# Quarter 3 of the feed-forward weights split in the feed-forward, and the routing's last steps reordered

## The chip, the cores and the metric

The kernel runs on one core of a Trainium2 chip. Its engines work side by side, each with an instruction queue of its own: TensorE (PE), VectorE (DVE), ScalarE (ACT), GpSimd (POOL) and SyncE (SP, which only issues transfers). They wait for each other by semaphores. The metric is the device time of one execution in microseconds.

## The reference

Two layers on `x` (4 batches of 512 rows of 512), each with a residual:

```python
x = x + gat(ctx_512, layernorm(x))                 # graph attention, the normed x as adjacency
x = x + moe(layernorm(x))                          # 8 experts, the best 2 per row, F = 352
x = x + softmax(norm(sim(layernorm(x), ctx @ Wk.T + bk)) * gamma + beta)
h = silu(x_n @ w_gate) * (x_n @ w_up)              # x_n = layernorm(x), I = 2048
x = x + sparsify_2to4(h) @ w_down                  # of every 4 neighbours the 2 largest stay
```

All products keep nearly fp32 precision: each operand is split in a high and a low part, and three products are summed (`product3`, L78 to L80).

## The kernel before

**Routing** (`gat_rows`, the end of its block). Batch by batch TensorE turns the rows (`turn_batch`, L254), multiplies them with the router's weights (`pe_logits`, L281) and counts rows per expert (`pe_count`, L418 and L422; the total is L426). VectorE takes the logits (`dve_logits`), chooses two experts per row (`dve_choose`; `keep`, L395), and behind the last batch makes the places (`dve_places`, from L449), a flag from bounds that TensorE has turned (L1103 to L1112), the token lists (`dve_tokens`, from L507) and the weights of the two experts (`dve_weights`, L435 to L445). GpSimd gathers the first rows (L528), and the block ends with a barrier of all engines.

**Expert stage** (`moe`). The rows come in 39 groups of 128, numbered 0 to 38. `pipeline` runs `body(g, ...)` for g from 1 to 38 on every engine. In a body TensorE makes the gate product of group g, turns the hidden values of g - 1, makes the up product, turns the rows of group g + 1 (L1629), and makes the down product of g - 1. So each L1629 marks one body: that at 154.56 us stands ahead of body 1, and those of bodies 4, 8, 12, 18, 22, 25, 26, 28 and 31 are shown among the rows below. ScalarE's order in a body is silu (L1711), high part of the hidden values (L1715), high part of the turned rows (L1719), result (L1724). Where the table says that a new expert begins soon, its raw weights are split: ScalarE makes the high parts (L1730), VectorE the low ones and the high part of the down weights (L1812, L1856), GpSimd the low part of the down weights (L1577). This happens in bodies 4, 8, 18, 21, 26 and 28.

Beside that work the weights of the feed-forward are split ahead of time. `w_scratch` holds high and low part of 16 rows of weights (4 quarters of 4), and each row is made in two chunks of 768 columns, 32 chunks in bodies 1 to 32. SP loads a raw chunk to one of four places of `pre_raw` (L1554), ScalarE writes its high part to one of two places of `pre` at the end of its body (`chunk_hi`, L1777), GpSimd subtracts (L1583) and issues the store (L1586):

```python
act.wait_ge(pre_kept[j % 2], 32 * i + 16 * (j // 2))     # the store of two chunks before
act.copy(pre[:, j % 2, 0, :], pre_raw[:, j, :]).then_inc(pre_hi, 1)
```

In bodies 29 to 38 the keys of the second layer's attention are made too; ScalarE's first cut stands behind the chunk of body 29 (L1756, L1758), VectorE takes the low part (`kv_c_lo`, L1850), and TensorE's key product stands in body 30.

**Feed-forward** (`ffn`). 16 units n, each one batch and one quarter of the inner width, in an order in which neighbours often share a quarter: `ORDER` gives (batch, quarter), `SPLIT` numbers the loads of a quarter, `FIRST` and `QUARTER` say at which unit a load is first used. Quarter 3 is first used in unit 3 (and again in unit 4, then in 9 and 14). Unit n has slots 6n to 6n + 5. In slots r = 0 to 3 TensorE makes gate and up of row r (`pe_gate_up`), in 4 and 5 the down product of unit n - 1 (`pe_down`). GpSimd fetches split weights from `w_scratch` to `f_w` (`fetch_gate_up` L1384, `fetch_down` L1393). ScalarE makes the silu (L1430), VectorE the product (L1436) and the choice of two in four (`keep_two`, L2650 to L2666), and both serve the attention of the other batches, whose steps `later_plan` sets into slots: `late` is the norm (L2014), `pre` and `post` are VectorE's part.

## Time and profile before

| | |
|---|---|
| median of 3 runs | 1042.15 us (1039.57 to 1042.34) |
| profiled execution | 1042.56 us, its span 1040.8 us |
| mean granted TensorE clock | 0.957 |
| busy share of the span | PE 92%, DVE 62%, ACT 38%, POOL 35% |
| moved | 195.56 MB, 188 GB/s |

The span runs from the first to the last instruction. A share of busy time is a mean over stages; TensorE's matmuls are pipelined. The chain is the work followed back from the last instruction, at each step to what released it. A timeline shows start, duration, engine, line, operation and, in brackets, how long the engine was idle before it and who ended that.

### The profile page before, as it was taken

The numbers are of one execution on the slowest core, as the hardware profiler recorded it, in microseconds if no ns is written. First come the engines' busy times: TensorE is split into PE (matmuls) and PEld (weight loads), VectorE is DVE, ScalarE is ACT, GpSimd is POOL, SyncE is SP. The second block draws the span as 40 slices with busy tenths as digits, with TensorE's granted clock in tenths as the row PEclk, the third lists the DMA queues.
The fourth block names the chain that finished last, engine by engine and source line by source line (L and its number), as shares of the span: only waits on it lengthen the run. The fifth ranks groups of instructions, "written<-read, shape, count | busy, mean of one in ns | idle before, by whom it ended". The sixth has DMA issues, their size and how long they took to land.

```text
span 1040.8 us, 15251 instructions
## 1 busy us (share of the span) xinstructions
PE 960.0 (92%) x4778; PEld 819.8 (79%) x4778; DVE 642.8 (62%) x1429; ACT 392.4 (38%) x697; POOL 360.4 (35%) x441
## 2 busy tenths in 40 slices
PE   4999639999989989858999999999999999999997
PEld 3889639889978888747788888888888888888885
DVE  7988644342432654465795876867858957665446
ACT  4875525444543533332332332422333324222121
POOL 0467026676576754733041220321311311101120
PEclk8998559999999999988999999999999999999999
DMA  9477349887789845364474334664263642545651
GB/s 340 168 147 162 121 132 339 315 305 279 250 304 325 296 178 158 101 207 149 160 238 167 102 111 152 215 222 130 68 216 122 202 162 81 171 154 163 201 146 57
DMA packets 68946, 195.56 MB, mean 188 GB/s; under 512 B 8176, under 2 KB 8304, under 8 KB 67632
## 3 DMA queue, kind: packets, MB, share of 16 engines
q0 software_dynamic: 41392, 129.78, 39.3%
q1 hardware_dynamic: 27456, 64.60, 17.8%
q8 instruction: 45, 0.74, 0.3%
q14 instruction: 53, 0.43, 0.1%
HBM read 146.38 MB, written 50.60 MB: 189 GB/s over the span
## 4 chain that ended last, share of the span: by engine, by line
PE 67%; DVE 6%; DMA 4%; issue 3%; POOL 3%; ACT 2%; DVEq 0%; ACTq 0%; POOLq 0%
PE ps L78 22%; PE ps L80 21%; PE ps L79 21%; DMA w_scratch<-pre 4%; POOL dn_w_lo L1577 2%; PE ps L1629 1%; PE ps L1989 1%; DVE gu_w_lo L1812 1%; POOL pre L1583 1%; DVE raw L2650 1%; PE ps L1657 1%; DVE raw L2666 1%; DVE dn_w_hi L1856 0%; ACT gu_w_hi L1730 0%; DVE m_hT_lo L1805 0%
## 5 line engine op out<-in xcount | busy, mean ns | idle before, releaser
L78 PE MATMUL ps<-f_x_lo,f_w 128*128 128x512 f32 (+1 forms) x524 | 203.2, 388 | 3.3 <-DVE raw L1436 1.7
L80 PE MATMUL ps<-f_x_hi,f_w 128*128 128x512 f32 (+1 forms) x524 | 202.3, 386 | 0.0
L79 PE MATMUL ps<-f_x_hi,f_w 128*128 128x512 f32 (+1 forms) x524 | 202.3, 386 | 0.0
L1430 ACT ACTIVATE moe_rows<-ps 128x512 f32<-128x512 f32 x64 | 38.3, 598 | 221.8 <-PE ps L80 221.7
L1436 DVE TENSOR_TENSOR raw<-moe_rows,ps 128x512 f32<-128x512 f32 x64 | 43.8, 685 | 120.1 <-PE ps L80 112.5
L78 PEld LDWEIGHTS ps<-f_x_lo,f_w 128*128 128x128 f32 x524 | 99.5, 190 | 23.5 <-DVE f_x_lo L2341 2.1
L80 PEld LDWEIGHTS ps<-f_x_hi,f_w 128*128 128x128 f32 x524 | 99.4, 190 | 19.5
L78 PE MATMUL ps<-gu_w_lo,m_xT_hi 128*128 (+1 forms) x312 | 106.0, 340 | 9.5 <-issue 5.7
L79 PEld LDWEIGHTS ps<-f_x_hi,f_w 128*128 128x128 f32 x524 | 99.5, 190 | 19.3
L78 PE MATMUL ps<-f_w,kv_c_hi 128*128 128x512 f32 x256 | 101.8, 398 | 2.3 <-DVE x L2685 2.3
L79 PE MATMUL ps<-gu_w_hi,m_xT_lo 128*128 (+1 forms) x312 | 101.9, 327 | 0.0
L80 PE MATMUL ps<-gu_w_hi,m_xT_hi 128*128 (+1 forms) x312 | 101.9, 327 | 0.0
L79 PE MATMUL ps<-f_w,kv_c_lo 128*128 128x512 f32 x256 | 101.1, 395 | 0.0
L80 PE MATMUL ps<-f_w,kv_c_hi 128*128 128x512 f32 x256 | 101.0, 395 | 0.0
L1805 DVE TENSOR_TENSOR m_hT_lo<-ps,m_hT_hi 128x384 fp32r<-128x384 f32 x39 | 21.7, 555 | 115.1 <-ACT m_hT_hi L1715 106.4
L1393 POOL DMA_DIRECT2D f_w<-w_scratch x52 | 37.0, 715 | 131.0 <-PE ps L80 130.2
L1384 POOL DMA_DIRECT2D f_w<-w_scratch x52 | 38.0, 732 | 116.6 <-PE ps L80 110.7
L1583 POOL TENSOR_TENSOR pre<-pre_raw,pre 128x768 fp32r<-128x768 f32 x32 | 58.9, 1840 | 44.6 <-ACT pre L1777 44.5
L78 PEld LDWEIGHTS ps<-gu_w_lo,m_xT_hi 128*128 128x128 f32 x312 | 59.7, 191 | 15.9 <-issue 9.3
L2685 DVE TENSOR_TENSOR x<-ps,x 128x512 f32<-128x512 f32 x64 | 42.8, 684 | 40.4 <-PE ps L80 40.4
L2650 DVE TENSOR_TENSOR raw<-kv_c_raw 128x768 bf16<-128x768 f32 (+2 forms) x96 | 60.3, 683 | 2.1 <-ACT kv_c_raw L2577 2.1
L79 PEld LDWEIGHTS ps<-gu_w_hi,m_xT_lo 128*128 128x128 f32 x312 | 60.1, 193 | 0.4
(368 smaller groups left out, 2007.3 us busy)
## 6 DMA issues: line engine op xcount, KB each, us to landing
f_w<-w_scratch POOLq DMA_DIRECT2D x52, 1024.0 KB, 5.7
f_w<-w_scratch POOLq DMA_DIRECT2D x52, 512.0 KB, 4.8
w_scratch<-pre POOLq DMA_DIRECT2D x32, 768.0 KB
pre_raw<-in_ffn SPq DMA_DIRECT2D x32, 384.0 KB
raw<-in_moe_gu SPq DMA_DIRECT2D x32, 352.0 KB
y_scratch<-m_y SPq DMA_DIRECT2D x39, 256.0 KB
raw<-in_moe_dn SPq DMA_DIRECT2D x24, 256.0 KB
x<-in_x SPq DMA_DIRECT2D x4, 1024.0 KB, 11.7
```

What stands on the lines that cost most here:

```text
L78: eng.matmul(out, lhs_hi, rhs_lo, start=start, stop=False)
L79: eng.matmul(out, lhs_lo, rhs_hi, start=False, stop=False)
L80: return eng.matmul(out, lhs_hi, rhs_hi, start=False, stop=stop)
L1384: pool.dma_start(self.w[r][:, :, 0:2, :], self.store[RQ * QUARTER[s] + r, :, :, 0:2, :]).then_inc(self.got_gu[r], 16)
L1393: pool.dma_start(self.w[r][:, :, k, :], self.store[RQ * QUARTER[s] + r, :, :, 2, :]).then_inc(got[r], 16)
L1430: act.activation(sg[:, k % 2, :], self.gate_bank(n, r), ACT.Silu).then_inc(self.silu, 1)
L1436: dve.tensor_tensor(out, sg[:, k % 2, :], self.up_bank(n, r), ALU.mult).then_inc(self.hid_made, 1)
L1577: pool.tensor_tensor(rt["dn_w_lo"][:, at], rt["raw_dn"], rt["dn_w_hi"][:, at].bitcast(F32), ALU.subtract).then_inc(dn_lo, 1)
L1583: pool.tensor_tensor(pre[:, k, 1, :], pre_raw[:, j, :], pre[:, k, 0, :].bitcast(F32), ALU.subtract).then_inc(pre_lo, 1)
L1805: dve.tensor_tensor(hT_lo[:, k, :, :], HB.rearrange("p (r n) -> p r n", r=RE), hT_hi[:, k, :, :].bitcast(F32), ALU.subtract).then_inc(h_lo ...
L2650: ins = dve.tensor_tensor(beats[:, at:at + w, :], mag[:, i, :].unsqueeze(1).broadcast_to([P, w, HN]), mag[:, j0:j1, :], ALU.is_ge)
L2685: dve.tensor_tensor(X[:, t, :], u.acc(n, i), X[:, t, :], ALU.add).then_inc(u.acc_free, 1)
```

## The change

In the routing, batch 2 is turned ahead of count 0, and counts 1 to 3 come behind the last logits. The softmax weights are scaled per batch (`dve_scale`), three times in `dve_places` ahead of the wait for the total and once behind it; `limits` (the flag) goes ahead of the last batch's logits, and `dve_weights` ahead of `dve_tokens`. In the expert stage 24 chunks remain, quarters 0 to 2, in the bodies of `SPLITS`. Quarter 3 is split in the feed-forward in six pieces: SP loads raw weights to one of three stages, ScalarE copies the high part straight to `f_w`, VectorE subtracts, and SP stores the pair to `w_scratch` for the later uses. The gate and up pieces stand in slots 1 to 4 of unit 2, the down pieces in slots 1 and 2 of unit 4. GpSimd no longer fetches quarter 3 for units 3 and 4. ScalarE's piece stands behind `late` in its slot (in slot 4 behind `size`), VectorE's behind `post` (in slot 4 at the unit's end).

```diff
-CHUNKS, CW = 2 * Q * RQ, 3 * D // 2
+CHUNKS, CW = 2 * RQ * (Q - 1), 3 * D // 2
+FRESH = (Q - 1,)
...
+    def dve_scale(self, chain, c):
+
+        dve, link = chain.eng, chain.link
+        s = slice(TB * c, TB * c + TB)
+        dve.wait_ge(self.exped, c + 1)
+        link(dve.tensor_tensor(self.ex[:, s, :], self.keep[:, s, :], self.ex[:, s, :], ALU.mult))
+        link(dve.tensor_reduce(self.den[:, s], self.ex[:, s, :], AX.X, ALU.add))
+        link(dve.reciprocal(self.den[:, s], self.den[:, s]))
+        dve.tensor_tensor(self.tw[:, s, :], self.ex[:, s, :], self.den[:, s].unsqueeze(2).broadcast_to([P, TB, E]),
+                          ALU.mult).then_inc(self.scaled, 1)
...
-        dve.wait_ge(self.exped, B)
-        link(dve.tensor_tensor(self.ex[:, :, :], self.keep[:, :, :], self.ex[:, :, :], ALU.mult))
-        link(dve.tensor_reduce(self.den[:, :], self.ex[:, :, :], AX.X, ALU.add))
-        link(dve.reciprocal(self.den[:, :], self.den[:, :]))
-        link(dve.tensor_tensor(self.tw[:, :, :], self.ex[:, :, :], per_e(self.den[:, :]), ALU.mult))
+            ins = dve.tensor_tensor(at[:, :, :], at[:, :, :], self.pos2[:, :, k].unsqueeze(2).broadcast_to([P, T, E]),
+                                    ALU.is_equal)
+        link(ins)
+        dve.wait_ge(self.scaled, B)
...
+        for c in range(B - 1):
+            self.dve_scale(chain, c)
         dve.wait_ge(self.counted, 1)
...
+                turn_batch(2)
+                lo.pe_logits(pe, 2)
                 rank.pe_count(pe, 0)
                 pe.wait_ge(bounds_ready, 1)
                 for j in range(4):
                     ins = pe.transpose(BOUNDS[:, P * j:P * j + P], per_part[:, j:j + 1], ident[:, :])
                 ins.then_inc(bounds_turned, 1)
-                turn_batch(2)
-                lo.pe_logits(pe, 2)
-                rank.pe_count(pe, 1)
                 turn_batch(3)
                 lo.pe_logits(pe, 3)
-                rank.pe_count(pe, 2)
-                rank.pe_count(pe, 3)
+                for c in range(1, B):
+                    rank.pe_count(pe, c)
                 rank.pe_index(pe)
...
+                    if c == B - 1:
+                        limits()
                     lo.dve_logits(dve, c)
                     rank.dve_choose(chain, c)
                 rank.dve_places(chain)
-                dve.wait_ge(bounds_turned, 1)
-                dve.tensor_reduce(red[:, 0:1], BOUNDS[:, 0:P], AX.X, ALU.min)
-                dve.tensor_reduce(red[:, 1:3], BOUNDS[:, P:3 * P].rearrange("p (k n) -> p k n", k=2), AX.X, ALU.add)
-                link(dve.tensor_reduce(red[:, 4:8], BOUNDS[:, 3 * P:4 * P].rearrange("p (k n) -> p k n", k=4), AX.X,
-                                       ALU.max))
-                link(dve.tensor_reduce(red[:, 8:10], red[:, 4:8].rearrange("p (k n) -> p k n", k=2), AX.X, ALU.add))
-                link(dve.tensor_tensor(red[:, 1:3], red[:, 1:3], red[:, 8:10], ALU.mult))
-                link(dve.tensor_scalar(red[:, 3:5], red[:, 1:3], BOUND_MAX, None, ALU.is_le))
-                link(dve.tensor_tensor(red[:, 3:4], red[:, 3:4], red[:, 4:5], ALU.mult))
-                link(dve.tensor_tensor(red[:, 3:4], red[:, 3:4], red[:, 0:1], ALU.mult))
-                dve.tensor_copy(flag[:, :], red[:, 3:4])
+                rank.dve_scale(chain, B - 1)
+                rank.dve_weights(chain)
...
+    def pieces(n, slot):
+
+        down = (("down", n - 1, slot - 1),) if n - 1 in FRESH and slot <= RQ // 2 else ()
+        gate_up = (("gate_up", n + 1, slot - 1),) if n + 1 in FRESH else ()
+        return down + gate_up
...
+    def load_piece(self, sp, piece):
+        kind, s, i = piece
+        at, t = self.place[piece], RQ * QUARTER[s]
+        if at >= 3:
+            sp.wait_ge(self.raw_lo, at - 2)
+        if kind == "gate_up":
+            sp.dma_start(self.stage[at % 3], self.raw[t + i][:, 0:2 * D]).then_inc(self.raw_got[at % 3], 16)
+        else:
+            sp.dma_start(self.piece_stage(piece), self.raw[t + 2 * i:t + 2 * i + 2, :, 2 * D:3 * D].rearrange("r p n -> p r n")
+                         ).then_inc(self.raw_got[at % 3], 16)
+
+    def keep_piece(self, sp, piece):
+        kind, s, i = piece
+        t = RQ * QUARTER[s]
+        sp.wait_ge(self.raw_lo, self.place[piece] + 1)
+        if kind == "gate_up":
+            sp.dma_start(self.store[t + i, :, :, 0:2, :], self.w[i][:, :, 0:2, :].bitcast(F32)).then_inc(self.kept_gu[i], 16)
+        else:
+            for r in (2 * i, 2 * i + 1):
+                sp.dma_start(self.store[t + r, :, :, 2, :], self.w[r][:, :, 2, :].bitcast(F32)).then_inc(self.kept_dn[r], 16)
+
+    def act_piece(self, act, piece):
+        kind, s, i = piece
+        at, stage = self.place[piece], self.piece_stage(piece)
+        act.wait_ge(self.raw_got[at % 3], 16 * (at // 3) + 16)
+        if kind == "gate_up":
+            act.wait_ge(self.products, RQ * (FIRST[s] - 1) + i + 1)
+            act.copy(self.w_hi[i][:, 0:2, :], stage).then_inc(self.raw_hi, 1)
+        else:
+            act.wait_ge(self.acc_done, TB * FIRST[s])
+            for k, r in enumerate((2 * i, 2 * i + 1)):
+                ins = act.copy(self.w_hi[r][:, 2, :], stage[:, k, :])
+            ins.then_inc(self.raw_hi, 1)
+
+    def dve_piece(self, dve, piece):
+        kind, s, i = piece
+        stage = self.piece_stage(piece)
+        dve.wait_ge(self.raw_hi, self.place[piece] + 1)
+        if kind == "gate_up":
+            dve.tensor_tensor(self.w_lo[i][:, 0:2, :], stage, self.w_hi[i][:, 0:2, :].bitcast(F32), ALU.subtract
+                               ).then_inc(self.raw_lo, 1)
+        else:
+            for k, r in enumerate((2 * i, 2 * i + 1)):
+                ins = dve.tensor_tensor(self.w_lo[r][:, 2, :], stage[:, k, :], self.w_hi[r][:, 2, :].bitcast(F32),
+                                         ALU.subtract)
+            ins.then_inc(self.raw_lo, 1)
...
+        SPLITS = {1 + 4 * m // 3: m for m in range(CHUNKS)}
+        LOADS = {g - 3: m for g, m in SPLITS.items() if g > 3}
...
-                if g <= CHUNKS:
-                    split_chunk(g, j, i)
+                if g in SPLITS:
+                    split_chunk(SPLITS[g])
...
+            order = list(u.place)
+            sp.wait_ge(first.sim_done, TB)
+            for piece in order[:2]:
+                u.load_piece(sp, piece)
+            for k, piece in enumerate(order):
+                if k + 2 < len(order):
+                    u.load_piece(sp, order[k + 2])
+                u.keep_piece(sp, piece)
```

Two of the three stages, `fresh_raw`, lie where `kv_wk_raw` and the first key lie before; the third is the end of `raw`. The first loads wait for the first batch's last similarity product.

## Rows read from the trace of the kernel before

**Rows 1.** Windows: length, busy PE, PEld, DVE, ACT, POOL, PEclk, DMA share, GB/s

```profile
148.00:440.00 292.00, 273.38 (x1575) 249.60 (x1575) 116.62 (x173) 126.71 (x227) 180.37 (x198) 0.98 0.75 261
...
516.00:1015.00 499.00, 499.00 (x2255) 411.43 (x2255) 344.69 (x804) 148.41 (x229) 105.29 (x145) 1.00 0.50 158
```

**Rows 2.** The page's chain, shares by engine and line

```profile
PE ps L78 22%; PE ps L80 21%; PE ps L79 21%; DMA w_scratch<-pre 4%; POOL dn_w_lo L1577 2%; PE ps L1629 1%; PE ps L1989 1%; DVE gu_w_lo L1812 1%; POOL pre L1583 1%; DVE raw L2650 1%; PE ps L1657 1%; DVE raw L2666 1%; DVE dn_w_hi L1856 0%; ACT gu_w_hi L1730 0%; DVE m_hT_lo L1805 0%
```

**Rows 3.** Timeline of PE, L1629: bodies 4, 8, 12, 18, 22, 25, 26, 28, 31

```profile
181.34 0.60 PE L1629 MATMUL ps<-ident,moe_rows 128*128 128x128 f32 x4
...
210.79 0.60 PE L1629 MATMUL ps<-ident,moe_rows 128*128 128x128 f32 x4
...
239.25 0.60 PE L1629 MATMUL ps<-ident,moe_rows 128*128 128x128 f32 x4
...
279.52 0.60 PE L1629 MATMUL ps<-ident,moe_rows 128*128 128x128 f32 x4
...
311.21 0.60 PE L1629 MATMUL ps<-ident,moe_rows 128*128 128x128 f32 x4
...
332.98 0.60 PE L1629 MATMUL ps<-ident,moe_rows 128*128 128x128 f32 x4
...
339.65 0.60 PE L1629 MATMUL ps<-ident,moe_rows 128*128 128x128 f32 x4
...
353.14 0.60 PE L1629 MATMUL ps<-ident,moe_rows 128*128 128x128 f32 x4
...
382.36 0.66 PE L1629 MATMUL ps<-ident,moe_rows 128*128 128x128 f32 x4 [0.32 <-DVE k_first L1840]
```

**Rows 4.** Chain behind body 26; ScalarE's waits before L1777; the last one

```profile
345.94 3.50 POOL dn_w_lo L1577
...
349.44 1.82 POOL pre L1583
...
351.55 9.08 DMA w_scratch<-pre
...
  DMA w_scratch<-pre: 17.3, 5
...
360.71 0.83 ACT L1777 CAST pre<-pre_raw 128x768 fp32r<-128x768 f32 x1 [4.25 <-DMA w_scratch<-pre]
```

**Rows 5.** Timeline of PE: the key product of body 30

```profile
370.47 0.50 PE L78 MATMUL ps<-kv_c_lo,kv_wk_hi 128*128 128x512 f32 x1 [2.50 <-DVE kv_c_lo L1850]
```

**Rows 6.** Timelines of PE, DVE and POOL at the end of the routing

```profile
117.88 0.64 PE L418 MATMUL ps<-g_keep,g_before_p 128*128 128x32 f32 x2 [1.11 <-DVE g_keep L395]
...
115.06 0.19 DVE L287 COPY logits<-ps 128x32 f32<-128x32 f32 x1 [3.26 <-PE ps L281]
...
120.65 0.29 DVE L451 TENSOR_TENSOR g_above<-ps,g_steps 128x128 f32<-128x128 f32 x1 [2.25 <-PE ps L426]
...
130.65 0.27 DVE L1103 TENSOR_REDUCE g_red<-ps 1x1 f32<-1x128 f32 x1
...
132.48 0.18 DVE L507 COPY g_tok_sum<-ps 128x39 f32<-128x39 f32 x1
...
135.65 0.27 DVE L445 TENSOR_REDUCE weight<-g_high 128x16 f32<-128x128 f32 x1
...
134.18 1.08 POOL L528 DMA_INDIRECT moe_rows<-xn_scratch,moe_index  x1 [0.17 <-issue]
```

**Rows 7.** Timelines of ACT and DVE in unit 2

```profile
554.77 0.58 ACT L1430 ACTIVATE moe_rows<-ps 128x512 f32<-128x512 f32 x1
...
563.36 1.07 ACT L2577 ACTIVATE kv_c_raw<-raw 128x1024 f32<-128x1024 f32 x1
...
545.79 0.69 DVE L2672 TENSOR_TENSOR kv_c_lo<-raw,kv_c_hi 128x512 fp32r<-128x512 f32 x1
...
555.44 0.69 DVE L1436 TENSOR_TENSOR raw<-moe_rows,ps 128x512 f32<-128x512 f32 x1 [2.64 <-ACT moe_rows L1430]
...
561.76 0.69 DVE L1436 TENSOR_TENSOR raw<-moe_rows,ps 128x512 f32<-128x512 f32 x1 [4.10 <-PE ps L80]
```

More of the change, by code:

```diff
@@ L1360, in __init__ @@
         self.acc_done, self.acc_free = sem(tag + "acc_done"), sem(tag + "acc_free")
+        self.raw = outer["dram"]["ffn"]
+        self.stage = [outer["raw"][:, 4 * D:6 * D]] + [outer["fresh_raw"][:, k, :] for k in range(2)]
+        self.raw_got = [sem(f"{tag}raw_got{k}") for k in range(3)]
+        self.raw_hi, self.raw_lo = sem(tag + "raw_hi"), sem(tag + "raw_lo")
+        self.kept_gu, self.kept_dn = ([sem(f"{tag}kept_{name}{r}") for r in range(RQ)] for name in ("gu", "dn"))
+        self.place = {}
@@ new lines, in __init__, with piece_stage @@
+        for n in range(UNITS):
+            for slot in range(1, RQ + 1):
+                for piece in self.pieces(n, slot):
+                    self.place[piece] = len(self.place)
+    @staticmethod
+    def pieces(n, slot):
+        down = (("down", n - 1, slot - 1),) if n - 1 in FRESH and slot <= RQ // 2 else ()
+        gate_up = (("gate_up", n + 1, slot - 1),) if n + 1 in FRESH else ()
+        return down + gate_up
+    def piece_stage(self, piece):
+        return self.stage[self.place[piece] % 3].rearrange("p (k n) -> p k n", k=2)
@@ new lines, in piece_tiles @@
+    def piece_tiles(self, piece):
+        kind, s, i = piece
+        return ((i, 0), (i, 1)) if kind == "gate_up" else ((2 * i, 2), (2 * i + 1, 2))
+    def load_piece(self, sp, piece):
[8 more added lines that the diff above has]
+                         ).then_inc(self.raw_got[at % 3], 16)
@@ new lines, in dve_piece @@
+    def dve_piece(self, dve, piece):
+        kind, s, i = piece
+        stage = self.piece_stage(piece)
[8 more added lines that the diff above has]
+            ins.then_inc(self.raw_lo, 1)
@@ new lines, in loads, with wait_gate_up, wait_down @@
+    @staticmethod
+    def loads(s):
+        return s + 1 - sum(f <= s for f in FRESH)
+    def wait_gate_up(self, pe, n, r):
+        s = SPLIT[n]
+        if s in FRESH:
+            pe.wait_ge(self.raw_lo, self.place["gate_up", s, r] + 1)
+        else:
+            pe.wait_ge(self.got_gu[r], 16 * self.loads(s))
+    def wait_down(self, pe, n, r):
+        s = SPLIT[n]
+        if s in FRESH:
+            pe.wait_ge(self.raw_lo, self.place["down", s, r // 2] + 1)
+        elif self.down_at(n) == 2:
+            pe.wait_ge(self.got_dn[r], 16 * self.loads(s))
+        else:
+            pe.wait_ge(self.got_last[r], 16)
@@ L1503, in pipeline, with chunk, chunk_pair @@
                 body(g, (g - 1) % 4, (g - 1) // 4)
-        def chunk(store, i, j):
-            return store[2 * i + j // 2][:, CW * (j % 2):CW * (j % 2) + CW]
-        def chunk_pair(store, i, j):
-            return store[2 * i + j // 2][:, :, CW * (j % 2):CW * (j % 2) + CW]
+        def chunk(m):
+            return dram["ffn"][m // 2][:, CW * (m % 2):CW * (m % 2) + CW]
+        def chunk_pair(m):
+            return outer["w_store"][m // 2][:, :, CW * (m % 2):CW * (m % 2) + CW]
+        SPLITS = {1 + 4 * m // 3: m for m in range(CHUNKS)}
+        LOADS = {g - 3: m for g, m in SPLITS.items() if g > 3}
         def kvT(b):
@@ L1565, in moe_sync @@
                 sp.sem_inc(stored[k], 16)
-            for c in range(3):
-                sp.dma_start(pre_raw[:, c, :], chunk(dram["ffn"], 0, c)).then_inc(pre_ld[c], 16)
+            for m in range(3):
+                load_chunk(m)
             reload(1)
@@ L2512, in ffn_gpsimd @@
                 for s in new(n - 1):
-                    if s >= 1:
+                    if s >= 1 and s not in FRESH:
                         for r in range(RQ):
@@ L2518, in ffn_gpsimd @@
                     for s in new(n + 1):
-                        u.fetch_gate_up(pool, s, r)
+                        if s not in FRESH:
+                            u.fetch_gate_up(pool, s, r)
                     if r < RQ - 1:
@@ L2584, in round_hid, with split_pieces @@
                     act.copy(hid_hi[:, r, :], hid[:, r, :]).then_inc(u.hid_hi_done, 1)
+            def split_pieces(n, slot):
+                for piece in u.pieces(n, slot):
+                    u.act_piece(act, piece)
             first.act(act)
@@ L2685, in evac, with split_pieces @@
                     dve.tensor_tensor(X[:, t, :], u.acc(n, i), X[:, t, :], ALU.add).then_inc(u.acc_free, 1)
+            def split_pieces(n, slot):
+                for piece in u.pieces(n, slot):
+                    u.dve_piece(dve, piece)
             first.dve(dve, chain)
```

88 lines of the change are left out of this document (52 added, 36 removed).

## The prediction

> **What bounds the kernel now.** I read four views, in this order. The windows cut the span into stages [rows 1]. From 516 to 1015 us, the feed-forward stage, TensorE is busy for the whole 499 us at full clock; in the expert stage (148 to 440) it is busy 273.4 of 292 us. So the long stage can only lose time, and the expert stage can give some. The page's chain says what is waited for there: 4% of the span, some 42 us, lies on stores of split weights to `w_scratch` [rows 2]. The turns of the next group's rows (L1629), one in each body of the expert loop, show where this costs [rows 3]: bodies 12 to 17 take 40.27 us, 6.71 each, and that is the undisturbed period. A new expert is split in bodies 4, 8, 18, 21, 26 and 28, and behind these the bodies are longer. Last, the chain behind body 26 and ScalarE's waits give the mechanism [rows 4].
>
> **The expert stage, before.** In body 26 (turn at 339.65) GpSimd subtracts the expert's down weights (345.94, 3.50 us), then its chunk (1.82); the store starts at 351.55, 11.9 behind the turn, and takes 9.08 to land. There are two `pre` buffers, so ScalarE's chunk two bodies on, in body 28, waits for it: 4.25 us before 360.71. The silu of the next group is queued behind that wait, and TensorE behind the silu. There are 5 such waits, 17.3 us in sum [rows 4], one for each split but the last.
>
> What they cost TensorE, from the turns [rows 3], at 6.71 a body: bodies 4 to 7, 29.45 less 26.85 = 2.6; 8 to 11, 28.46 less 26.85 = 1.6; 18 to 21, 31.69 less 26.85 = 4.8; 22 to 24, 21.77 less 20.14 = 1.6; 26 to 30, 42.71 less 33.56 = 9.15, of which I count 1.3 as work (a key product of three such matmuls as at 370.47, and a key turn), so 7.8. In sum 18.5 us. Without the 2.50 us that TensorE waits for `kv_c_lo` [rows 5] that is 16.0, about one for one with ScalarE's 17.3.
>
> **Expert stage, after.** The 24 chunks stand in bodies 1 + 4m//3 (rounded down), so bodies 4, 8, 12 to 32 have none. Splits 4, 8 and 28 have no chunk behind them. GpSimd is then free at 9.8 us behind the split body's turn (349.44 less 339.65), gathers for the next body (1.08 as in [rows 6] and two small instructions, 1.7 in all) and subtracts the next chunk by 13.4; the store starts near 13.8 and at 9.08 lands by 22.9. The next user of the buffer is three bodies behind the split. ScalarE wants it 3.3 behind that body's turn (as body 28: 360.71 less 4.25 against 353.14), so at 23.4: no wait, with 0.5 to spare. For splits 18 and 26, which keep their chunk, the next user is also three bodies on (21, 29): landing 11.9 + 9.1 = 21.0 against 23.4. Split 21 alone has a user two bodies on: 21.0 against 16.7, a wait of 4.3 in body 23. I charge 4.0 for it, the price of the one wait of that length (bounds 1.6, what its bodies lose now, and 4.8, the most that a split's bodies lose for one such wait). The wait for `kv_c_lo` stays, since ScalarE cuts the key behind body 29's chunk, which still exists: 2.5 [rows 5]. So 6.5 of the 18.5 remain: **minus 12.0**. Bounds: minus 7.8, if the 0.5 to spare is missed behind splits 4 and 8 (their 4.2 stay); minus 14.4, if split 21 costs 1.6. The chunks that are gone from other bodies give nothing, since TensorE sets the period there.
>
> **Routing.** Batch 2 is turned before count 0, so count 1 leaves the way to batch 3's logits and joins count 2 behind them. TensorE's work is the same; what it can win is its wait for batch 3's `keep`, 1.11 us before 117.88 [rows 6]; I take 0.9. Three of the four new weight scalings (12 instructions of 128x32, at 0.22, below the 0.29 of the 128x128 one at 120.65) are 2.7 us in VectorE's wait for the total, 2.25 now; it grows by the 1.2 that the earlier logits add, to 3.5. The limits (130.65 to 132.48, 1.8) move into its wait for batch 3's logits, 3.26 before 115.06. Without these covers they would cost 2.7 and 1.8 on the way to the total. Behind the places now come the fourth scaling (0.9) and the `weight` instructions, which stood behind the tokens (two compares, two products and two sums, 1.3): from 129.75 to 132.0. The tokens then start 0.5 before the 132.48 of now, and VectorE ends with them near 132.9 and not at 135.9 [rows 6]. The last into the block's barrier is then GpSimd's gather (134.18 and 1.08 long, less 0.4), at 134.9. So **minus 1.0** for all that stands behind the barrier; bounds 0, if something that no row shows sets it (an engine's own start there), and minus 2.
>
> **The feed-forward stage.** Quarter 3's first use loads no split weights. In unit 2 come four copies of 128x1024 on ScalarE (1.07 each, the row of that width [rows 7]) and four subtractions on VectorE (1.38, twice the 0.69 of 128x512 [rows 7]); in unit 4 two pieces of twice 128x512, costed alike. In sum 6.4 us of ScalarE and 8.3 of VectorE. GpSimd's queue loses eight loads. SP gets six reads and eight stores; what is queued behind them there is the output store of unit 5, which nothing waits for before the end. The tightest place is the silu at 554.77 [rows 7]: it waits for a late norm, and a piece now stands between the two. The silu comes 1.1 later, VectorE's product (555.44) 1.8 later. VectorE waits 2.64 us before that product and 4.10 before the next [rows 7], and TensorE needs it only behind the next gate and up, 6 us later. So nearly hidden: **plus 0.3**, bounds 0 and 3 (one piece's 1.07 + 1.38 shown, and 0.5 in unit 4). The first three reads, 1.5 MB, start near 465, ahead of loads with work before them: 0, or 1 as a bound.
>
> A rule bears on the moved subtractions. The 0.69 us was measured with GpSimd not computing. The Trainium skill, "SBUF — State Buffer", section "Who interferes with whom", says that a VectorE instruction with two SBUF inputs is blocked by a GpSimd instruction that reads SBUF. By it each of the six pieces may first wait out a GpSimd instruction; at no more than 1.08, as long as the gather of [rows 6], and all in the open, the sum would be 1036 and not 1030. The trace of now has no moved piece to show it.
>
> **The sum.** The profiled execution took 1042.56 us, 1.76 more than its span of 1040.8, and lies 0.4 above the median of 1042.15. 1042.56 - 12.0 - 1.0 + 0.3 = 1029.9; against the median 1029.5. I say 1030. The bounds in sum: 1026 (-14.4, -2, 0) and 1039 (-7.8, 0, +4).
>
> **The rivals.**
> (a) The waits move: stores started behind splits 4, 8 and 18 still land too late. 2.6 + 1.6 + 4.8 stay, the expert stage gives 3.0: about 1039. For it: a margin of 0.5 under landings of 9 us. Against it: fewer chunks are in flight. If only the 4.2 stays, 1034. Chance 0.15, nearly all for the milder.
> (b) Slower: the pieces are not hidden. TensorE has no idle time in units 2 to 4, and each gate and up pair has two waits, for the silu's bank and for the product's; a piece that shows in one costs 2.45, in both 4.9. Six pieces: 14.7 to 29.4, the middle 22 gives 1052. It decides from 12.7 us, from 15.8 for more than 0.3% over now. Against it: the 2.64 and 4.10 in that very unit and VectorE at 69% of the stage [rows 1]. 0.06.
> (c) A transfer decides: kept stores and raw reads from SP delay a weight load that TensorE waits for. One load late by as much as a store takes, 9.08 [rows 4], gives 1039. Against it: the engines' share is 0.50 in that stage [rows 1]. 0.06. The Trainium skill, "DMA: Bandwidth & Descriptors", section "Issuing engines are not separate DMA queues", has all queues on the same 16 engines.
> (d) The change doesn't do what it could: TensorE's lost 18.5 us come from the expert split itself (3.50 on GpSimd), which is untouched. Then only routing is won, 1041.5. Against it: ScalarE's waits name the store. 0.06.
> My forecast: 0.67.
>
> **How the numbers follow.** A measurement can tell 0.3%, 3.1 us: faster is below 1039.0. The forecast (0.67), (a) without its worst (0.14) and half of (c) (0.03) are: 0.84. Same: (d), the rest of (a) and (c): 0.10. Slower: (b), 0.06. The likeliest case's own range is 1026 to 1034. That for 8 in 10 takes in the milder (a) and most of the way to the upper bound: 1025 to 1038.
>
> **What would show it.** After: the stores fall to about 1% of the chain; ScalarE's chunk waits for a store once, in body 23, some 4 us; turns 6.7 apart from body 1 to 21, longer stretches only at 22 to 24 and at 30. The last instructions of VectorE before the barrier are the tokens', and the first turn of expert rows comes 1 us earlier. TensorE shows no idle time in units 2 to 5, and the new copies take 1.07, the subtractions 1.4. The prediction is wrong if the waits behind splits 4, 8, 18 and 26 are still there, or if TensorE idles in the feed-forward stage.

## The result and the profile after

| | before | after |
|---|---|---|
| median of 6 executions, us | 1042.24 (1039.57 to 1044.08) | 1033.73 (1027.64 to 1035.66) |
| ratio, 95% interval | | 0.9909 [0.9887, 0.9931] |
| profiled execution, its span, us | 1042.56, 1040.8 | 1035.23, 1033.2 |

The change made the kernel 8.5 us faster; the forecast was 12. The 7.3 us between the two profiled executions are a sum of unlike parts: the expert stage gave 13.8, the routing took 5.7, the stretch behind the experts, nearly all of it feed-forward, took 0.4, and the time outside the span 0.3. Executions more than 1.5% above the fastest of their kernel are counted as slow and left out of medians and ratios, which touches only e1 below (two of its ten, 1050.3 and 1051.6 us). In the kernel after, the products are L79 to L81, the row turns L1738, a chunk's copy L1886, its subtraction L1693 and its store L1696.

**The expert stage.** The chain of the page. The stores (`w_scratch<-pre`) had 4% in [rows 2] and have 1% now; gathers of rows, which had no entry, have 2%:

```profile
PE ps L79 23%; PE ps L81 22%; PE ps L80 22%; DMA moe_rows<-xn_scratch,moe_index 2%; PE ps L1738 1%; POOL dn_w_lo L1687 1%; PE ps L2098 1%; PE ps L1766 1%; DVE raw L2775 1%; DMA w_scratch<-pre 1%; DVE gu_w_lo L1921 1%; DVE raw L2791 1%; POOL pre L1693 1%; DVE x L2810 0%; DVE x L2487 0%
```

Windows of TensorE over the expert stage and the feed-forward stage (columns: length, busy (count), PEclk, DMA share, GB/s), as [rows 1]. TensorE's idle time in the expert stage fell from 18.6 us of 292 to 9.8 of 278. In the feed-forward there is still none:

```profile
155.00:433.00 278.00, 268.18 (x1576) 0.99 0.69 241
509.00:1015.00 506.00, 506.00 (x2286) 1.00 0.49 159
```

Turns of bodies 1, 4, 8, 12, 18, 20, 21, 22, 24, 25, 26, 28, 29, 30 and 31, as [rows 3]:

```profile
167.16 0.60 PE L1738 MATMUL ps<-ident,moe_rows 128*128 128x128 f32 x4
...
187.24 0.60 PE L1738 MATMUL ps<-ident,moe_rows 128*128 128x128 f32 x4
...
214.04 0.60 PE L1738 MATMUL ps<-ident,moe_rows 128*128 128x128 f32 x4
...
240.80 0.60 PE L1738 MATMUL ps<-ident,moe_rows 128*128 128x128 f32 x4
...
281.27 0.60 PE L1738 MATMUL ps<-ident,moe_rows 128*128 128x128 f32 x4
...
294.62 0.60 PE L1738 MATMUL ps<-ident,moe_rows 128*128 128x128 f32 x4
302.87 0.66 PE L1738 MATMUL ps<-ident,moe_rows 128*128 128x128 f32 x4 [0.24 <-DMA moe_rows<-xn_scratch,moe_index]
309.88 0.60 PE L1738 MATMUL ps<-ident,moe_rows 128*128 128x128 f32 x4
...
323.24 0.60 PE L1738 MATMUL ps<-ident,moe_rows 128*128 128x128 f32 x4
331.84 0.60 PE L1738 MATMUL ps<-ident,moe_rows 128*128 128x128 f32 x4
338.51 0.60 PE L1738 MATMUL ps<-ident,moe_rows 128*128 128x128 f32 x4
...
351.96 0.60 PE L1738 MATMUL ps<-ident,moe_rows 128*128 128x128 f32 x4
360.56 0.66 PE L1738 MATMUL ps<-ident,moe_rows 128*128 128x128 f32 x4 [0.88 <-DMA moe_rows<-xn_scratch,moe_index]
370.24 0.60 PE L1738 MATMUL ps<-ident,moe_rows 128*128 128x128 f32 x4
377.87 0.66 PE L1738 MATMUL ps<-ident,moe_rows 128*128 128x128 f32 x4 [0.35 <-DVE k_first L1949]
```

At 6.71 a body: 4 to 7 now 26.80 (29.45 before), 8 to 11 26.76 (28.46), so splits 4 and 8 cost nothing any more. The long ones are 20 to 21 (8.25), 24 to 25 (8.60), 28 to 29 (8.60) and 29 to 30 (9.68). Lost are 1.8 in bodies 18 to 21, 1.8 in 22 to 24 and 4.5 in 26 to 30 (39.36, less 33.56, less 1.3 of work): 8.1 of the former 18.5.

Three causes stand behind these. ScalarE waits for a store once, in body 23 (ScalarE's wait before L1886), and TensorE still waits for the key's operand, as in [rows 5]:

```profile
322.14 0.83 ACT L1886 CAST pre<-pre_raw 128x768 fp32r<-128x768 f32 x1 [2.28 <-DMA w_scratch<-pre]
```

```profile
367.53 0.50 PE L79 MATMUL ps<-kv_c_lo,kv_wk_hi 128*128 128x512 f32 x1 [1.79 <-DVE kv_c_lo L1959]
```

The third is new to the account. It is the chain that ends in the turn of body 21:

```profile
287.56 3.49 POOL dn_w_lo L1687
291.04 1.82 POOL pre L1693
...
293.15 0.72 POOL w_scratch L1696
...
294.50 8.33 DMA moe_rows<-xn_scratch,moe_index
...
302.87 0.67 PE ps L1738 x4
```

GpSimd's queue holds the split of body 18, then that body's chunk and store, and only then the gather of the rows that TensorE turns in body 21. The gather starts late and takes 8.33 us (median of the 39 gathers: 4.6). The turn of body 29 waits 0.88 in the same way behind split 26. The kernel before had this too, at three turns, the longest ahead of the turn of body 21:

```profile
302.22 0.66 PE L1629 MATMUL ps<-ident,moe_rows 128*128 128x128 f32 x4 [1.96 <-DMA moe_rows<-xn_scratch,moe_index]
```

**The routing.** TensorE, VectorE and GpSimd, as [rows 6]: first one batch's logits, the third product of counts, then VectorE around the scalings, and the gather.

```profile
92.97 6.84 PE L282 MATMUL ps<-g_gw_centred,g_w_raw 128*128 128x8 f32 x32
...
123.95 0.61 PE L419 MATMUL ps<-g_keep,g_before_p 128*128 128x32 f32 x2
...
126.09 0.58 PE L427 MATMUL ps<-g_ksum,g_ones 128*128 128x8 f32 x2
```

```profile
119.87 0.19 DVE L288 COPY logits<-ps 128x32 f32<-128x32 f32 x1 [1.81 <-PE ps L282]
...
126.70 0.29 DVE L459 TENSOR_TENSOR g_above<-ps,g_steps 128x128 f32<-128x128 f32 x1 [1.20 <-PE ps L427]
...
136.70 0.18 DVE L434 TENSOR_TENSOR g_ex<-g_keep,g_ex 128x32 f32<-128x32 f32 x1
...
138.91 0.19 DVE L515 COPY g_tok_sum<-ps 128x39 f32<-128x39 f32 x1
```

```profile
140.23 1.08 POOL L536 DMA_INDIRECT moe_rows<-xn_scratch,moe_index  x1 [0.27 <-issue]
```

The 1.11 us wait before count 3 is gone, the scalings and the limits lie in VectorE's waits (1.20 and 1.81 left of them). Yet the gather starts at 140.23 and not at 134.18, since two of the four batches' 32 logits products took 6.84 and 6.83 us at a granted clock of 0.50.

**The feed-forward.** A piece's subtraction on VectorE and its copy on ScalarE:

```profile
554.75 1.22 DVE L1439 TENSOR_TENSOR f_w<-fresh_raw,f_w 128x1024 fp32r<-128x1024 f32 x1
```

```profile
551.82 1.04 ACT L1427 CAST f_w<-fresh_raw 128x1024 fp32r<-128x1024 f32 x1
```

### The profile page after: what moved, and what is told of

It reads as the page before. It is cut to its first block, busy times and chain, and to the rows that moved or that the text cites. A ratio compares the mean times of both kernels' runs of the same rounds, so it can differ in the third digit from the quotient of the medians.

```text
span 1033.2 us, 15319 instructions
## 1 busy us (share of the span) xinstructions
PE 961.6 (93%) x4778; PEld 825.2 (80%) x4778; DVE 650.8 (63%) x1449; ACT 391.4 (38%) x697; POOL 333.6 (32%) x417
## 4 chain that ended last, share of the span: by engine, by line
PE 71%; DVE 6%; issue 2%; DMA 2%; POOL 2%; ACT 1%; DVEq 0%; ACTq 0%; POOLq 0%
PE ps L79 23%; PE ps L81 22%; PE ps L80 22%; DMA moe_rows<-xn_scratch,moe_index 2%; PE ps L1738 1%; POOL dn_w_lo L1687 1%; PE ps L2098 1%; PE ps L1766 1%; DVE raw L2775 1%; DMA w_scratch<-pre 1%; DVE gu_w_lo L1921 1%; DVE raw L2791 1%; POOL pre L1693 1%; DVE x L2810 0%; DVE x L2487 0%
## 5 line engine op out<-in xcount | busy, mean ns | idle before, releaser
L79 PE MATMUL ps<-f_x_lo,f_w 128*128 128x512 f32 (+1 forms) x524 | 203.6, 389 | 3.3 <-DVE raw L1543 1.7
L81 PE MATMUL ps<-f_x_hi,f_w 128*128 128x512 f32 (+1 forms) x524 | 202.6, 387 | 0.0
L79 PEld LDWEIGHTS ps<-f_x_lo,f_w 128*128 128x128 f32 x524 | 99.6, 190 | 23.6 <-issue 2.1
L81 PEld LDWEIGHTS ps<-f_x_hi,f_w 128*128 128x128 f32 x524 | 99.5, 190 | 19.5
L79 PE MATMUL ps<-gu_w_lo,m_xT_hi 128*128 (+1 forms) x312 | 105.2, 337 | 7.0 <-issue 4.5
L79 PE MATMUL ps<-f_w,kv_c_hi 128*128 128x512 f32 x256 | 101.9, 398 | 2.3 <-DVE x L2810 2.3
L81 PE MATMUL ps<-gu_w_hi,m_xT_hi 128*128 (+1 forms) x312 | 101.5, 325 | 0.0
L81 PE MATMUL ps<-f_w,kv_c_hi 128*128 128x512 f32 x256 | 101.1, 395 | 0.0
L1503 POOL DMA_DIRECT2D f_w<-w_scratch x48 | 34.2, 715 | 130.1 <-PE ps L81 130.1
L1492 POOL DMA_DIRECT2D f_w<-w_scratch x48 | 35.1, 732 | 110.0 <-PE ps L81 106.2
L79 PEld LDWEIGHTS ps<-gu_w_lo,m_xT_hi 128*128 128x128 f32 x312 | 59.5, 191 | 12.7 <-issue 7.0
L1693 POOL TENSOR_TENSOR pre<-pre_raw,pre 128x768 fp32r<-128x768 f32 x24 | 44.2, 1840 | 48.1 <-ACT pre L1886 47.8
```

What stands on the lines that cost most here:

```text
L79: eng.matmul(out, lhs_hi, rhs_lo, start=start, stop=False)
L81: return eng.matmul(out, lhs_hi, rhs_hi, start=False, stop=stop)
L1492: pool.dma_start(self.w[r][:, :, 0:2, :], self.store[RQ * QUARTER[s] + r, :, :, 0:2, :]).then_inc(self.got_gu[r], 16)
L1503: pool.dma_start(self.w[r][:, :, k, :], self.store[RQ * QUARTER[s] + r, :, :, 2, :]).then_inc(got[r], 16)
L1693: pool.tensor_tensor(pre[:, k, 1, :], pre_raw[:, m % 4, :], pre[:, k, 0, :].bitcast(F32), ALU.subtract).then_inc(pre_lo, 1)
```

## The experiments

There are twelve runs. Each was profiled once, and all but e4 and e12 were also timed against executions of the kernel before on the same chip (e1 to e4 on one, e5 to e8 on a second, e9 to e12 on a third). The second table reads one profile of each; "experts" is from the first expert product to the first product of the next stage's attention, "rest" from there to the end of TensorE's last product.

| kernel | median, us (executions) | ratio to before, 95% |
|---|---|---|
| e1 routing part alone | 1039.05 (8) | 0.9945 [0.9913, 0.9977] |
| e2 weights part alone | 1034.92 (6) | 0.9911 [0.9884, 0.9939] |
| e3 the change again | 1034.26 (6) | 0.9891 [0.9862, 0.992] |
| e5 six chunks moved | 1032.64 (6) | 0.9882 [0.9847, 0.9916] |
| e6 one chunk moved | 1034.97 (6) | 0.9895 [0.9859, 0.993] |
| e7 before, third buffer | 1040.8 (12) | 0.9954 [0.9926, 0.9982] |
| e8 pieces twice | 1040.44 (12) | 0.997 [0.9946, 0.9994] |
| e9 before, chunks left out | 1033.35 (6) | 0.9899 [0.9867, 0.9931] |
| e10 six chunks moved, again | 1029.06 (6) | 0.9859 [0.982, 0.9899] |
| e11 the change, third time | 1029.51 (6) | 0.9871 [0.9832, 0.991] |

| profile | its time | logits of batches 0 to 3 | first expert product | experts | rest |
|---|---|---|---|---|---|
| before | 1042.56 | 3.90 3.92 3.77 4.11 | 148.75 | 302.7 | 585.8 |
| e4 (before) | 1040.17 | 4.02 4.04 3.89 3.99 | 149.56 | 299.8 | 585.5 |
| e12 (before) | 1040.69 | 3.71 6.84 4.00 3.88 | 150.97 | 298.1 | 586.3 |
| e1 | 1038.65 | 5.26 3.72 3.74 3.77 | 149.80 | 297.5 | 586.0 |
| after | 1035.23 | 4.71 6.84 6.83 4.37 | 154.45 | 288.9 | 586.2 |
| e2 | 1035.40 | 4.96 4.01 6.84 6.83 | 155.94 | 287.8 | 586.0 |
| e3 (after) | 1038.44 | 6.97 4.05 6.83 3.84 | 156.48 | 290.5 | 585.8 |
| e11 (after) | 1029.32 | 5.03 3.94 3.84 3.99 | 149.53 | 288.4 | 585.7 |
| e5 | 1034.27 | 5.96 6.83 6.83 4.01 | 159.72 | 283.5 | 585.4 |
| e10 (as e5) | 1024.96 | 4.96 4.01 3.92 4.07 | 148.91 | 284.4 | 586.0 |
| e6 | 1037.02 | 4.72 6.83 6.83 4.39 | 156.63 | 288.6 | 586.2 |
| e7 | 1032.64 | 4.03 4.05 3.90 3.98 | 149.90 | 290.7 | 586.7 |
| e8 | 1038.25 | 3.71 6.83 6.83 4.35 | 154.61 | 288.9 | 589.0 |
| e9 | 1032.08 | 5.60 3.99 3.84 4.04 | 151.84 | 289.3 | 585.6 |

**e1 and e2: each part alone.** e1 is the kernel before with all edits of the routing (`dve_scale`, the order of turns and counts, `limits`, the places of weights and tokens) and none of the weights'; e2 the reverse.

> The kernel before with the routing's part of the change alone. In the profile of the changed kernel TensorE's clock stayed at half level (0.50) from 88 to 112 us, and the 32 router products of a batch took 6.8 us where they took 3.9 before; the first expert product came 5.7 us later (154.45 against 148.75). Theory A, the new order of TensorE's work lowers the clock: this kernel is about 5 us slower than before (ratio 1.005), with the first expert product near 154 us. Theory B, the clock there changes from one execution to the next whatever the order, and the parts' own work gains 0.5 to 1 us: the ratio is 0.999 within its interval, and the times of single executions spread over 5 to 8 us as those of both kernels do.

> The kernel before with the weights' part of the change alone (24 chunks in the expert stage, six pieces in the feed-forward, the routing as before). Theory A (order lowers the clock): the whole gain of 13.7 us that the expert stage shows, ratio 0.987, 4 to 5 us better than the full change. Theory B (chance): the same as the full change within 1 us if the routing's edit is worth nothing, ratio 0.991. Both: expert stage 278 to 279 us long from the first product to the last, and the feed-forward from 508 to 1024 us without idle TensorE time.

e2 has nearly all of the change's gain, as its theory B said. e1 missed its expectation of 0.999: it was timed 0.55% faster than before, and the interval leaves 0.999 out. Its profile shows no more than 1.1 us for the routing (next section), and the two parts' ratios multiplied give 0.986, more than the whole change has. What the rest of e1's gain is stays open. e2, with the old order of the routing, has two batches' logits at 6.8 us, and e1, with the new order, none. So it is not the new order that brings the half clock.

**e3, e4, e11, e12: the two kernels as they are, once more.** No edit.

> The changed kernel once more, for a second profile and five more times. Theory A: the clock in the routing is at half level from 88 to 112 us again, first expert product near 154 us. Theory B: another pattern of the clock is possible, with the first expert product anywhere from 147 to 155 us, and the time of the profiled execution moves with it: 1028 to 1036 us.

> The kernel before once more, for a second profile. Theory A: the clock alternates as in the first profile (0.57, 0.85, 0.50, 0.79 in stretches of 4 us from 88 us), first expert product near 148.8 us. Theory B: it may stay at half level in this profile, with the first expert product up to 6 us later and the time up to 1044 us.

> The changed kernel as it is. Median 1033 to 1036 us, ratio to before 0.989 to 0.992. Clock in the routing: if it belongs to this kernel, two or three of the four batches' logits products take 6.8 us again; if it is chance, 3.8 to 4.1 us is as likely.

> The kernel before as it is, one look at the clock in the routing: if it belongs to the kernel, all four batches' logits products take 3.8 to 4.1 us and the first expert product starts at 149 to 150 us; if it is chance, half clock in some of them.

e3's profile (first expert product at 156.48, 1038.44 us) lies beyond the ranges of both its theories. After ten profiles the half clock seemed to belong to the weights part: six of six with it, none of four without. e11 and e12 undid that. TensorE's logits in the changed kernel (e11), and one batch's in the kernel before (e12):

```profile
86.00 5.03 PE L282 MATMUL ps<-g_gw_centred,g_ctx_raw 128*128 128x8 f32 x32 [1.37 <-DVE g_ybuf L1010]
...
94.33 3.94 PE L282 MATMUL ps<-g_gw_centred,g_w_raw 128*128 128x8 f32 x32
...
101.37 3.84 PE L282 MATMUL ps<-g_gw_centred,g_ctx_raw 128*128 128x8 f32 x32
...
111.31 3.99 PE L282 MATMUL ps<-g_gw_centred,g_w_raw 128*128 128x8 f32 x32
```

```profile
90.92 6.84 PE L281 MATMUL ps<-g_gw_centred,g_w_raw 128*128 128x8 f32 x32
```

The same changed kernel has 6.8 us in two batches or in none, and e10 and e5, which are one kernel, start their experts at 148.91 and 159.72. It varies from execution to execution. With all four batches near full clock the changed kernel took 1029.3 us. The median of e11's six executions, 1029.51, is below what was expected of it: between one set of six and the next the same kernel's median moved by over 4 us.

**e5 and e10: no chunk in a body with an expert's split.**

```
-SPLITS = {1 + 4 * m // 3: m for m in range(CHUNKS)}
+AT = {12: 16, 13: 17, 14: 19, 15: 20, 18: 24, 19: 25}
+SPLITS = {AT.get(m, 1 + 4 * m // 3): m for m in range(CHUNKS)}
```

> The changed kernel with six of its 24 chunks at other bodies (16, 17, 19, 20, 24, 25 in place of 17, 18, 19, 21, 25, 26), so that no chunk stands in a body that splits an expert's down weights (4, 8, 18, 21, 26, 28). Theory A, that what is left over in the expert stage comes from a chunk standing behind such a split on GpSimd: ScalarE's only chunk wait (2.28 us at body 23) is gone, the late gathers before the turns of bodies 21 and 29 are gone, the periods of bodies 21, 25 and 29 fall from 8.25, 8.60 and 8.60 us to about 6.8, and first product to last down product falls from 278.4 to about 273.5 us; ratio to the changed kernel about 0.995, to the kernel before about 0.985. Rival B, that the body is long because of the expert's split itself: the periods stay over 8 us and the stage within 1 us of 278.4.

> The changed kernel with six chunks at other bodies, once more, to be compared on one chip with the changed kernel. In the profile all bodies up to 30 took 6.7 us and first product to last down product is 5 us shorter than in the changed kernel; theory A gives a median 3 to 6 us below the changed kernel's of the same call; if the executions' own spread hides it, the difference is within 2 us.

Turns of bodies 1 and 29 in e5, and in the kernel before:

```profile
172.47 0.60 PE L1739 MATMUL ps<-ident,moe_rows 128*128 128x128 f32 x4
...
360.12 0.60 PE L1739 MATMUL ps<-ident,moe_rows 128*128 128x128 f32 x4
```

```profile
161.17 0.60 PE L1629 MATMUL ps<-ident,moe_rows 128*128 128x128 f32 x4
...
361.75 0.66 PE L1629 MATMUL ps<-ident,moe_rows 128*128 128x128 f32 x4 [0.41 <-DMA moe_rows<-xn_scratch,moe_index]
```

That is 187.65 us for 28 bodies, 6.70 each, against 193.40 after and, by the same turns, 200.58 before: up to the turn of body 29 no body is long any more, no chunk waits and TensorE waits for no gather. The stage is 283.5 and 284.4 us against 287.8 to 290.5. The splits themselves, which are all still there, cost TensorE nothing. What stays long is the stretch from the turn of body 29 to that of 30, 9.93 us, with the wait for the key's operand (2.28); in e10 it is 11.35, part of it half clock (last section). In the timings the gain over the changed kernel is not clear: e10 and e11, on one chip, are 0.5 us apart, and all 12 executions of this kernel have a median of 1030.7 against 1033.1 for all 18 of the changed one, less than the spread of either. Its ratio to before, 0.9882 and 0.9859, is the lowest here.

**e6: one chunk moved**, from body 21 to 20 (`AT = {15: 20}`).

> The changed kernel with one chunk alone moved, from body 21 (where GpSimd splits an expert's down weights) to body 20, where none is. Theory A, two causes: ScalarE's wait of 2.28 us for the chunk's store at body 23 goes and with it 1.5 to 2.3 us of the stage (278.4 to about 276.5), while the late gather before the turn of body 21, which stands behind the chunk of body 18, and the one before the turn of body 29 stay. Rival B: the wait moves to the chunk of body 22 (its buffer's last store is now one body earlier, so this needs another late store) and the stage stays within 0.5 us.

Rival B's numbers came: the stage is 288.6 us, and ScalarE's wait did not go but is in body 20 now:

```profile
302.21 0.83 ACT L1887 CAST pre<-pre_raw 128x768 fp32r<-128x768 f32 x1 [2.09 <-DMA w_scratch<-pre]
```

The chunk of body 20 uses the buffer whose store stands behind split 18, one body less far away than before. But the moved wait is not what kept the stage long. The stretch up to the turn of body 21, late before as well, is 8.04 us (8.25 before the edit). The one up to the turn of body 25 fell from 8.60 to 6.67, so by 1.9, inside theory A's 1.5 to 2.3. What ate that up lies later: the stretches up to the turns of bodies 29, 30 and 31 grew by 0.3, 1.2 and 0.3, and behind the key's wait TensorE ran at half clock here, as the changed kernel did in none of its three profiles (windows of TensorE):

```profile
368.00:370.00 2.00, 2.00 (x9) 0.74 0.76 317
370.00:372.00 2.00, 2.00 (x9) 0.50 0.67 211
```

From the key's first product to the turn of body 30 it took 3.98 us, in the changed kernel 2.71. So theory A holds for the bodies, and the stage's sum hid it.

**e7: the kernel before with a third buffer.** All 32 chunks, the old order.

```
+THIRD = 27
+buffer = [m % 3 if m < THIRD else (m - THIRD) % 2 for m in range(CHUNKS)]
-act.wait_ge(pre_kept[j % 2], 32 * i + 16 * (j // 2))
+act.wait_ge(pre_kept[k], 16 * buffer[:m].count(k))
```

> The kernel before, all 32 chunks, with a third buffer for a chunk's two parts (in turn up to chunk 26, two buffers for the last five), so that a store has a whole body more to land. Theory A, that the expert stage before was long by ScalarE's wait for a store that GpSimd had issued late, and that fewer chunks gave back just that: the waits behind the splits of bodies 4, 8, 12 to 22 go, first product to last down product falls from 292.2 to 281 to 284 us, and the time to about 1033 (ratio to the kernel before 0.990 to 0.993). Rival (d), that the time is lost by the split itself or by the number of chunks: 290 us or more, ratio 0.998 or more.

No chunk of ScalarE waits for a store, and the stage falls to 290.7 us from 297.5 to 302.7 in the four profiles with the chunks as before. By the turns, counted as in the prediction, the bodies behind the splits still lose 10.5 us of the former 18.5 (1.7, 0.6, 2.1, 3.0 and 3.1). So the waits for the stores, with what followed from them, were 8 us, less than half, and the number of chunks was not what counted. What is left is the other cause. Two of four such turns:

```profile
204.10 0.66 PE L1634 MATMUL ps<-ident,moe_rows 128*128 128x128 f32 x4 [1.41 <-DMA moe_rows<-xn_scratch,moe_index]
...
322.87 0.66 PE L1634 MATMUL ps<-ident,moe_rows 128*128 128x128 f32 x4 [1.70 <-DMA moe_rows<-xn_scratch,moe_index]
```

TensorE waits 5.0 us in all at four turns for gathers that stand behind a split and a chunk. The profiled execution took 1032.64, but the median of 12 is 1040.8, and the ratio of 0.9954 misses the 0.990 to 0.993 of theory A as well as the 0.998 of the rival. The stage decides for A, on one profile; the timings alone do not (see the clock, last section).

**e8: each piece's work done twice** (copy and subtraction, the first result overwritten).

```
+act.copy(self.w_lo[i][:, 0:2, :], stage)
 act.copy(self.w_hi[i][:, 0:2, :], stage).then_inc(self.raw_hi, 1)
...
+link(dve.tensor_tensor(self.w_lo[i][:, 0:2, :], stage, self.w_hi[i][:, 0:2, :].bitcast(F32), ALU.subtract))
```

> The changed kernel with each piece's copy on ScalarE and subtraction on VectorE done twice in units 2 to 5 of the feed-forward (the first result is overwritten by the second). Theory A, that this work lies wholly beside TensorE's: the feed-forward stays at 515.6 us within 0.5, with no idle time of TensorE in these units, ratio to the changed kernel within 0.997 to 1.003. Rival (b), that a piece's work is on the path where it is not covered: up to 14.7 us more, ratio 1.014.

Neither theory: of some 14 us more work (by the rows' durations 6.6 on ScalarE and 7.6 on VectorE) TensorE sees 2.8, nearly all in two waits:

```profile
555.88 0.39 PE L79 MATMUL ps<-f_x_lo,k_hi 128*128 128x256 f32 x1 [1.87 <-DVE f_x_lo L2180]
...
627.27 0.39 PE L79 MATMUL ps<-k_lo,k_hi 128*128 128x256 f32 x1 [0.61 <-DVE k_lo L2180]
```

Both are for a split of the attention that stands behind a piece on VectorE, and neither for the silu or the product that the rival named. Done once, the pieces cost TensorE no wait at all; done twice, they nearly fit. The median of 12, 1040.44, is 7 us above the 1033.1 of all the changed kernel's executions; the profile shows 2.8 of that, and the rest stays open.

**e9: the kernel before with eight chunks left out.** The feed-forward fetches quarter 0's weights in the place of quarter 3's, so it moves the same bytes and its result is not the reference's.

```
-if g <= CHUNKS:
+if g <= CHUNKS and g % 4 != 0:
```

> The kernel before with eight of its 32 chunks left out, those of bodies 4, 8, ..., 32, and nothing in their place: the feed-forward fetches all from the scratch tensor as before, and in the place of quarter 3's weights it fetches those of quarter 0, so that quarter's contribution is not the reference's. The order and the spacing of the other 24 chunks are those of the changed kernel, the routing is that of before, and there are no pieces. Theory A, the gain is the expert stage's alone and the pieces cost nothing: first product to last down product 278 to 279 us, feed-forward 515.6, time as the changed kernel's within 0.3%. Rival: the time is below the changed kernel's by more than 0.3% because the pieces or the order of the routing cost something. On TensorE's clock in the routing: of the ten profiles so far the six of kernels with the weights part ran two to three of the four batches' 32 logits products at 6.8 us (half clock), the four without it none. If the feed-forward's added code goes with that, this kernel shows the logits at 3.8 to 4.1 us and the first expert product at 149 to 150 us; if the 24 chunks go with it, 6.8 us and 154 to 160 us.

The expert stage is 289.3 us, as in the changed kernel, without any piece in the feed-forward; its rest is 585.6 and theirs 585.7 to 586.2. The median of 1033.35 is within 0.4 of the first one of the changed kernel and of the 1033.1 of all its executions, but 3.8 above e11's on the same chip. By the stages, the eight chunks alone make the gain, and the pieces that do their work elsewhere cost nothing that can be measured; the timings don't contradict it, but can't show it.

## Why the prediction was right, and where not

- *The mechanism is right, its share too large.* ScalarE's chunk waited for stores that GpSimd issued behind a split: e7 took the waits away without a chunk less, and e5 took them away with all splits in place. Rival (d) is out. But the prediction put 16.0 of the 18.5 us to these waits, "about one for one", and e7, which has none of them, still loses 10.5: they hid the late gathers. Of the 8.0 that went, 3.4 was half clock behind the waits in the profile before (last section).
- *Waits behind splits 4 and 8: 4.2 us.* Right; their bodies are at 6.70 and 6.69. Rival (a) is out, the milder one too.
- *Split 21 charged with 4.0.* The wait is in body 23, as said, but 2.28 us long and not 4.3, since its store landed in 7.23 and not 9.08; the bodies lost 1.8.
- *Splits 18 and 26 free.* Wrong. The reckoning asked for the store's next user alone. The gather of the rows that TensorE turns three bodies on stands behind the same chunk, and it was late in the kernel before too (1.96 us ahead of the turn of body 21, shown above), beside ScalarE's waits. It costs 1.8 behind split 18 and, with the key's wait (1.79; forecast 2.5), 4.5 in bodies 26 to 30.
- *The expert stage, -12.0.* By these bodies 18.5 - 8.1 = 10.4, inside the bounds. That it came so near is in part luck: of the 6.5 us left over by the forecast, split 21 was charged 2.2 too much and the key's wait 0.7, and the gathers behind splits 18 and 26, 1.8 and 2.7, not at all. Over the profiles the gain is the same: mean experts 299.5 us in the four with the old chunks, 288.9 in the five with the new (after, e2, e3, e8, e11), 10.6 less. Some 3 of these are not waits but half clock behind them, which the forecast did not have (last section). The 13.8 of the first pair has 3.2 more. They lie in bodies 36 and 37 of the kernel before, in two idle times with no releaser that none of its other two profiles has:

```profile
420.52 0.66 PE L1629 MATMUL ps<-ident,moe_rows 128*128 128x128 f32 x4 [1.43 <-issue]
...
424.90 0.42 PE L78 MATMUL ps<-gu_w_lo,m_xT_hi 128*128 x1 [1.63 <-issue]
```

- *Routing, -1.0.* The size is right, by another sum. From the first logits to the total the old order takes 35.4 us with all batches at full clock (before, e4, e7), and the new one 35.2 to 35.5 with a first batch that took 1.0 to 1.3 longer (e1, e10, e11): 1.1 less, the wait before count 3. The step "the tokens then start 0.5 before" failed: the fourth scaling and the weights took 2.2 (136.70 to 138.91) in the place of the limits' 1.8, so the tokens' copy comes 0.4 later behind the total, and the gather starts 14.1 behind it in every kernel. Nor was VectorE's end what the barrier waited for: before, it ended 0.66 behind the gather's instruction (135.92 against 135.26), now it ends ahead of the gather's start, and the first expert product comes 14.2 to 14.8 behind the gather's start in the profiles with the old order and 14.1 to 14.8 in those with the new. Behind the total nothing is won.
- *What the forecast did not have: the clock in the routing.* It took TensorE's work to be the same and so its time. Half clock in the logits makes 2.9 us a batch, 5.7 net in the profile after. e11, with three batches at full clock and most of the first, took 1029.3 against the forecast's 1030; against e4, the kernel before with all four at full clock, that is 10.9 less, where the forecast had 12.7.
- *Feed-forward, +0.3.* It was 0. The copies take 1.04 (forecast 1.07), the subtractions 1.22 (1.38). Rival (b) is out: even doubled, the pieces show 2.8 us on TensorE, and the stretch without any piece (e9) is as long as with them. Rival (c) is out: no load is waited for. The rule of the Trainium skill, "SBUF — State Buffer", "Who interferes with whom", which gave 1036, had nothing to bite on: GpSimd computes nothing next to the four gate and up pieces, and all four subtractions take 1.22 to 1.23.

## What to carry to other kernels

When work is queued on an engine behind a long instruction, list all that stands behind it, the gathers too, and ask for each how many bodies later it is needed. The longest wait hides the others. Moving the whole set off the loaded bodies (e5) made the stage even up to the key's product; moving one piece (e6) moved the wait and still shortened a body, which the stage's sum did not show. So read the single bodies, with the clock beside them. And a stage whose products run at one clock in one execution and at the other in the next can vary more between executions of one kernel than a change is worth, so compare stages and not spans.

## What the runs showed of the hardware

- **TensorE's clock in the routing.** While TensorE is busy without a gap on 128x8 products and 128x128 turns (4.00 of 4.00 us in each window from 88 to 112), the granted clock, as a mean over 4 us, is 0.50 to 0.85 in the kernel before and 0.50 throughout in the profile after, and it falls differently in each execution: 32 logits products take 3.7 to 4.1 us or 6.83, that is 2.4 or 1.2 GHz, or a time in between. The instructions and their order are the same. The Trainium skill, "TensorE: Matmul & The Clock Gate", Part 1, says that the activity monitor's window runs freely and is not reset when a kernel starts; the traces agree in so far as the same program falls on either side. Why it falls here at all, with TensorE busy, stays open.
- **The clock falls behind waits in the expert stage too.** In the kernel before, behind the waits at the turn of body 21 and at the key's product (2.50 us, [rows 5]):

```profile
304.00:306.00 2.00, 2.00 (x6) 0.50 0.77 296
...
372.00:374.00 2.00, 2.00 (x9) 0.50 0.98 397
```

  Between the turns of bodies 1 and 31 there are two such stretches in the profile before and in e4, one in e12 and in e1, and none in after, e2, e3, e8 and e11. One of them costs about 1.7 us (an estimate: one less the granted clock, summed over windows of 1 us), e4's longer one twice that. By it from the key's first product to the next turn is 4.27 us before and 2.71 after. That makes a mean of 3.0 us in the four old profiles, part of the 10.6. e6, e9 and e10 have one each, at the key. It does not follow from the wait's length alone: the clock fell behind 1.80 us in e6 and stayed at 1.00 behind 2.28 in e5.
- **It spreads the times.** The mean granted clock of an execution lies between 0.948 and 0.963, and times follow it. Of the kernel before, 13 executions at 0.957 or more have a median of 1042.2 us and 18 at 0.952 or less one of 1046.1; of e7, 1034.9 and 1042.3 (six each); of the changed kernel, 1029.7 (ten) and 1035.5 (three); of e5 and e10, 1025.8 (four) and 1032.8 (five). Compared within either group e7 gives 7.3 or 3.8 us, though its plain median is 3 us better, and e5 and e10 give 3.8 or 2.7 over the change. The groups mix chips and are small, so this is a hint and no proof.
- **A gather of 128 rows takes 4.6 us as a median, and the one behind split 18 took 8.33.** Such a gather is late by its issue and by its landing. The store just ahead of it does not explain the long landing: both it and the one of body 18, at 282.19, start 1.35 us behind a chunk's store, and that one landed in 3.75. The engines that move the data were busier under the two longest (8.33 at 294.50, 8.75 at 351.76) than under the short one (windows of GpSimd, from issue to landing; DMA share last but one), but others with a share of 0.92 landed in 4.6, so what makes a gather long stays open:

```profile
282.19:285.94 3.75, 1.02 (x1) 1.00 0.82 311
...
294.50:302.83 8.33, 6.40 (x9) 1.00 0.98 371
...
351.76:360.51 8.75, 8.07 (x7) 1.00 0.97 356
```
